# First LayerNorm of a two-layer block: statistics of blocks 2 to 7 moved from VectorE to ScalarE

## The reference, cut to what matters

```python
m = jnp.mean(x, axis=-1, keepdims=True)
v = jnp.var(x, axis=-1, keepdims=True)
xn = (x - m) / jnp.sqrt(v + 1e-5)
x = x + attention(xn) + ffn(xn)
```

## Time and profile before

| | |
|---|---|
| median of 3 runs | 1813.74 us (1809.82 to 1813.79) |
| the profiled execution's own time | 1823.78 us |
| its span on the core | 1821.9 us |
| mean granted TensorE clock | 0.942 of full speed |

### The profile page before, as it was taken

The page is one execution under the profiler, slowest core; times in us unless marked ns, Lnnn a source line. Parts: engine busy times, 40 slices in busy tenths (PEclk is TensorE's granted clock), DMA queues, the critical chain, the costliest instruction groups (busy, mean ns, idle before and its releaser), DMA issues.

```text
span 1821.9 us, 32039 instructions
## 1 busy us (share of the span) xinstructions
PE 1638.2 (90%) x10912; PEld 1214.3 (67%) x10912; DVE 869.7 (48%) x2492; ACT 667.7 (37%) x1617; POOL 738.1 (41%) x845
## 2 busy tenths in 40 slices
PE   3798988988887999999988578999899999999997
PEld 2344534444443799999755345656899999999997
DVE  3866787667650232322165797988322112222221
ACT  1344444445452122222353334432433333333332
POOL 3122223455551055555542237885233333333332
PEclk8789988989897999999999789999999999999999
DMA  7533433252404122222351255435622222222221
GB/s 203 117 90 95 97 84 76 54 106 64 95 5 163 66 72 72 71 73 70 117 162 58 73 174 117 97 70 123 240 36 36 38 36 39 36 36 35 37 40 22
DMA packets 79739, 149.98 MB, mean 82 GB/s; under 512 B 13125, under 2 KB 61377, under 8 KB 73441
## 3 DMA queue, kind: packets, MB, share of 16 engines
q1 hardware_dynamic: 55040, 110.56, 23.2%
q0 software_dynamic: 24544, 37.38, 9.5%
HBM read 103.05 MB, written 44.45 MB: 81 GB/s over the span
## 4 chain that ended last, share of the span: by engine, by line
PE 78%; DVE 12%; issue 4%; ACT 2%; DMA 2%; POOL 1%; SPq 0%; DVEq 0%; ACTq 0%; POOLq 0%
PE PS L1413 21%; PE PS L1431 20%; PE PS L1299 5%; DVE PS L1717 5%; PE PS L1237 3%; PE PS L1526 3%; PE PS L1378 3%; PE PS L1387 2%; PE PS L1263 2%; PE PS L1617 2%; PE PS L1398 2%; PE PS L1284 2%; PE PS L1325 2%; PE PS L1536 1%; PE PS L1606 1%
## 5 line engine op out<-in xcount | busy, mean ns | idle before, releaser
L1413 PEld LDWEIGHTS PS<-arena 128*128 128x128 f32 x3408 | 400.7, 193 | 15.8 <-DVE arena L1940 4.5
L1413 PE MATMUL PS<-arena 128*128 128x128 f32 x3408 | 407.5, 277 | 3.1 <-DVE arena L1940 3.1
L1431 PE MATMUL PS<-arena 128*128 x1704 | 392.4, 379 | 0.0
L1431 PEld LDWEIGHTS PS<-arena 128*128 128x128 f32 x1704 | 311.6, 190 | 40.2 <-issue 0.2
L1940 DVE COPY arena<-PS 128x256 f32<-128x256 f32 x142 | 60.3, 425 | 413.2 <-PE PS L1398 402.9
L1717 DVE CUSTOM_DVE_ANT_0 PS<-PS,arena 128x512 f32<-128x512 f32 (+3 forms) x512 | 234.2, 524 | 36.2 <-PE PS L1263 36.0
L866 POOL DMA_INDIRECT out<-arena x71 | 111.6, 1572 | 313.6 <-ACT arena L1087 292.5
L1077 ACT ACTIVATE arena<-PS,arena 128x128 f32<-128x128 f32 x568 | 162.4, 368 | 138.2 <-PE PS L1413 138.2
L1016 ACT ACTIVATE arena<-PS 128x512 f32<-128x512 f32 (+1 forms) x256 | 166.9, 704 | 89.0 <-PE PS L1284 87.8
L806 POOL TENSOR_SCALAR_AFFINE_SELECT arena<-arena 128x256 f32<-128x256 f32 x256 | 99.0, 411 | 230.8 <-ACT arena L1016 229.4
L852 POOL DMA_INDIRECT arena<-XN,arena x142 | 142.0, 1000 | 122.8 <-PE PS L1398 81.6
(11 more groups left out here) (237 smaller groups left out, 2058.5 us busy)
## 6 DMA issues: line engine op xcount, KB each, us to landing
arena<-FD SPq DMA_DIRECT2D x32, 512.0 KB
arena<-in_w SPq DMA_DIRECT2D x16, 1024.0 KB
SPL<-arena SPq DMA_DIRECT2D x32, 384.0 KB, 2.6
arena<-SPL SPq DMA_DIRECT2D x32, 384.0 KB, 5.3
XN<-arena SPq DMA_DIRECT2D x16, 512.0 KB, 2.9
arena<-SPL SPq DMA_DIRECT2D x32, 256.0 KB, 6.2
arena<-SUM SPq DMA_DIRECT2D x16, 512.0 KB, 5.1
arena<-in_x SPq DMA_DIRECT2D x8, 512.0 KB, 10.1
```

The costliest lines, as they stand in the source:

```text
L1413: ins = pe.matmul(o, m.now[i % 2][:, c * F + 128 * f:c * F + 128 * f + 128], m.xt[i % 2][:, 128 * c:128 * c + 128], start=(c == 0), stop=( ...
L1431: ins = pe.matmul(to, m.hT[i % len(m.hT)][:, 128 * c:128 * c + 128], m.WD[:, bass.ds(e * (nf * 256) + c * 256, 256)], start=(c == 0), stop ...
```

## The change

VectorE keeps the statistics of blocks 0 and 1. Those of blocks 2 to 7 are made by ScalarE at the same places of `plan0`: four `Copy` activations with scale 1/256, whose accumulated sum is the mean, a wait on its own semaphore `mean_made`, and four `Square` activations of `mean - x` (scale -1, the mean as a per-partition bias) whose accumulated sum is 256 times the variance. What the activations write goes to `OTT`, which holds nothing at that time. The last square root takes scale 1/256 to make up for it and waits on `square_made` in place of `stat`. The counts of `stat` fall by 12 in layer 1.

```diff
             def root0(k):
                 lo, hi = ((0, 4), (4, 8), (8, 32))[k]
-                act.wait_ge(stat, (2, 4, 16)[k])
+                if k < 2:
+                    act.wait_ge(stat, 2 * k + 2)
+                else:
+                    act.wait_ge(square_made, NB - 2)
                 act.wait_ge(const_set, 3)
-                act.activation(RS[:, lo:hi], MV[:, lo:hi, 1], ACT.Sqrt, bias=EPS[:, :]).then_inc(root)
+                act.activation(RS[:, lo:hi], MV[:, lo:hi, 1], ACT.Sqrt, bias=EPS[:, :], scale=1.0 if k < 2 else 1.0 / D).then_inc(root)
+
+            def stats0(n):
+
+                left = [OTT[j // 2][:, 256 * (j % 2):256 * (j % 2) + 256] for j in range(4)]
+                act.wait_ge(x_in[n], 16)
+                if n > 2:
+                    act.wait_ge(square_made, n - 2)
+                for j in range(4):
+                    i = 4 * n + j
+                    ins = act.activation(left[j], ACC[:, i, :], ACT.Copy, scale=1.0 / D, accum_out=MV[:, i, 0:1])
+                ins.then_inc(mean_made)
+                act.wait_ge(mean_made, n - 1)
+                for j in range(4):
+                    i = 4 * n + j
+                    ins = act.activation(left[j], ACC[:, i, :], ACT.Square, bias=MV[:, i, 0:1], scale=-1.0, accum_out=MV[:, i, 1:2])
+                ins.then_inc(square_made)
...
             for kind, *a in plan0:
-                if kind == "root":
+                if kind == "stats" and a[0] >= 2:
+                    stats0(*a)
+                elif kind == "root":
...
             for kind, *a in plan0:
-                if kind == "stats":
+                if kind == "stats" and a[0] < 2:
                     stats0(*a)
```

More of the change, by code:

```diff
@@ L500, in build @@
         stat = sem("stat")
+        mean_made, square_made = sem("mean_made"), sem("square_made")
         root = sem("root")
@@ L1113, in scalar @@
                     b = a[0]
-                    act.wait_ge(stat, 16 + 2 * b + 2)
+                    act.wait_ge(stat, 4 + 2 * b + 2)
                     act.activation(RS[:, 4 * b:4 * b + 4], MV[:, 4 * b:4 * b + 4, 1], ACT.Sqrt, bias=EPS[:, :]).then_inc(root)
@@ L1973, in stats1 @@
                 if b:
-                    dve.wait_ge(stat, 16 + 2 * b)
+                    dve.wait_ge(stat, 4 + 2 * b)
                 else:
@@ L1980, in stats1 @@
                 ins.then_inc(stat)
-                dve.wait_ge(stat, 16 + 2 * b + 1)
+                dve.wait_ge(stat, 4 + 2 * b + 1)
                 for j in range(4):
```

## The result

The changed kernel takes 1818.7 us in the median of 22 runs (1811.0 to 1824.5), the kernel before 1811.4 in 22 (1805.5 to 1817.3). The ratio is 1.0038, 95% interval 1.0027 to 1.0049: slower by 6.9 us, 4.9 to 8.9. The forecast was 7.9 us or 0.44%, and a time of 1821.6 us.

A forecast was written before the change was run, and what follows sets the result against it. VectorE bounds the changed stretch before; afterwards ScalarE's chain sets norm(2), 5.8 us later, plus 2.1 us waiting on TensorE's lowered clock: 7.9 us on 1813.7 gives 1821.6 us. Range for 8 in 10: 1815 to 1828.

The forecast's parts named there:

- What bounds the stretch: 60 to 90 us: VectorE bounds it before, 28.07 of 30 us busy; six blocks, 10.3 us, are the most saved.
- VectorE's relief wins: Rival: accumulations overlap so well that a block costs under 2.4 us; faster, at best 10.3 us off, 1803.4; chance 4%.
- Blocks 2 and 3 at no cost: Their 7.7 us fit ScalarE's 15.90 us idle before maxrow(0); block 2 brings the first rounding 1.72 us earlier, to 68.91.
- The price of a block: On ScalarE: four copies, four squares and the rounding of the rows, 3.85 us, against VectorE's 1.72.
- The chain: ScalarE's steps from the first rounding at 68.91, with blocks 4 to 7, put norm(2)'s subtraction at 93.29, +5.8 us.
- extra table load: Rival at blocks 6 and 7: square not in the exponential's table, four switches, 5.2 us more, 1826.8; chance 8%.
- The clock's term: After TensorE's idle stretch, about 73 to 79.6 us, its clock is lower; ScalarE waits 2.1 us for project_v's second copy.
- The sum: At norm(2): 5.8 + 2.1 = 7.9 us late, all of it reaching the end; 1821.6 us, 0.44% slower.
- A sign of being wrong: Behind norm(2): all spans should shift by a constant; a later stage starting less late would make the prediction wrong.
- absorption: Rival, behind norm(2) or by a cheap block: delay partly swallowed, 1815.7 to 1819.5 us; chance 24%.
- The point of no change: Block price on ScalarE at which norm(2) would be neither later nor sooner: 3.85 - 5.83 / 4 = 2.4 us.

The follow-up runs named there:

- two_three: Changed kernel with only blocks 2 and 3 on ScalarE, 4 to 7 back on VectorE: 1810.7 us, ratio 1.0000 to the kernel before.
- warm_longer: Changed kernel with TensorE's two idle stretches filled by 58 and 34 unused matmuls: 1821.8 us, ratio 1.0055 to the kernel before.
- again: The changed kernel unaltered, timed once more with a second trace: 1819.7 us, ratio 1.0050 to the kernel before.
- four_seven: Changed kernel with blocks 2 and 3 back on VectorE, 4 to 7 on ScalarE: 1824.3 us, ratio 1.0053 to the kernel before.
- warm: Changed kernel with TensorE's two idle stretches filled by 40 and 24 unused matmuls: 1820.0 us, ratio 1.0043 to the kernel before.
- squares_only: Changed kernel without the four copies, their wait and the bias, mean taken as 0: 1812.9 us, ratio 0.9998 to the kernel before.
- early4: Changed kernel with blocks 2 to 5 on ScalarE, all at block 2's place, 6 and 7 on VectorE: 1809.7 us, ratio 0.9983 to the kernel before.
- early3: Changed kernel with blocks 2 to 4 on ScalarE, all at block 2's place, 5 to 7 on VectorE: 1808.3 us, ratio 0.9980 to the kernel before.
- early3_again: early3 timed once more for a tighter interval: ratio 0.9991 to the kernel before.

## Why the prediction was right

- **What bounds the stretch.** As predicted, VectorE's relief did not count once ScalarE's chain was the longer one. The 10.3 us taken off VectorE turned into waits: the five between 66 and 96 us add up to 18.0 us (forecast: some 15), 4.46 at the reciprocal among them.
- **A misread chain, without effect on the sum.** The prediction says that the `bn_stats` of all six blocks stand in the chain of the kernel before. Five do. Block 3's, at 66.14, do not: there the chain runs over TensorE and ScalarE, and VectorE waits 1.51 us for the rounding:

```profile
62.05 1.27 DVE arena L1657 x4
...
66.28 0.60 PE PS L1271 x4
66.88 3.72 PE PS L1237 x4
70.63 0.61 ACT arena L993
71.26 0.70 DVE arena L1703
...
72.33 1.41 DVE arena L1657 x4
```

So at most five blocks, 8.6 us, could come off, and not the 10.3 of the rival "VectorE's relief wins". The forecast itself counts only block 2 ahead of the first rounding and adds up ScalarE's steps from there, so it did not need the wrong reading.
- **Blocks 2 and 3 at no cost.** Shown by two_three: -1.5 us at norm(2), forecast -1.7, and block 3 went into a wait. That they cost nothing is clear; how much block 2 gives is within the scatter of the traces ahead of it. That the first rounding stood at 68.91 to the hundredth was luck: maxrow(0) came 1.42 us sooner (65.50), not 1.72, the projection behind it took 3.48 us instead of 3.78, and in the second trace of the same kernel the rounding stood at 69.42.
- **The price of a block.** Forecast 3.85, measured 3.71. The pitch of the copies is 0.40 (0.41 forecast), of the squares 0.49 (0.50). Four blocks make it 0.6 us over. The durations alone have medians of 406 and 492 ns (24 each). The estimates worked out in the prediction from the Trainium skill (ScalarE: Activation LUTs, What ACT_TABLE_LOAD costs) were 399 and 492. The drain of 1.38 us at a switch, which that section also gives, is not in these rows: the load lasted 1.28 us from 92.74, right behind the exponentials, and the root ran at 94.03.
- **The chain.** Forecast 68.91, 73.27, load of the table 77.7, norm(2) 93.29 without the clock; measured 68.91, 73.11, 77.40, and 94.59 - 1.92 = 92.67. No extra table load appeared, so squares run behind an exponential without one; that rival is out. The kernel before spoke against it more than the prediction says: at 974.62 us layer 1's squares follow a Gelu activation (L1058, at 974.12, behind a table load at 972.83) without a load between.
- **The clock's term.** Forecast a wait of 2.1 us, measured 1.92 and, in a second execution, 0.93. warm_longer takes it away and norm(2) follows. So it is a real term of some 1 to 2 us, which depends on the execution; that the first trace met the forecast to 0.2 us is partly luck.
- **The sum.** 7.9 at norm(2), measured 7.1 there (6.7 in the second trace) and 6.9 in the whole (9.1 in the second set). Whether a delay at norm(2) reaches the end, all runs together say, in us against the kernel before:

| kernel | norm(2), one trace | the whole (95% interval) |
|---|---|---|
| changed | +7.1 | +6.9 (4.9 to 8.9) |
| again | +6.7 | +9.1 (6.3 to 11.8) |
| four_seven | +8.4 | +9.6 (6.2 to 13.0) |
| warm | +6.1 | +7.8 (4.9 to 10.7) |
| warm_longer | +5.6 | +10.0 (6.0 to 13.8) |
| squares_only | -0.3 | -0.4 (-4.2 to 3.4) |
| two_three | -1.5 | 0.0 (-3.1 to 3.3) |
| early4 | -2.3 | -3.1 (-6.2 to 0.0) |
| early3 | -4.7 | -3.6 (-6.7 to -0.4) |
| early3_again | -4.9 | -1.6 (-4.5 to 1.1) |

Late kernels are slow and early ones are not, and in eight of ten rows norm(2) lies inside the interval of the whole. So the delay reaches the end in the main, which is shown; to a microsecond or two it is not, and why warm_longer's 2 us did not show stays open.
- **A sign of being wrong that appeared.** The prediction calls itself wrong if a later stage starts less late than norm(2), and expects a constant shift. In the two first traces the last projection was only 5.5 us late and the first routed expert 0.4. I do not count it as absorption, because the medians are 7.3 apart and the second trace of the changed kernel differs from its own first by 5.0 us at that expert. The sign asked of two single traces what they could not tell.
- **What was off.** The profiled execution was to take 1831.7 us and took 1824.35. The reason is the scatter between executions, not the change: the trace of before was one of its slowest executions. A sum put on the median did not suffer from it; one put on the profiled execution did. The forecast of 1821.6 us was 2.9 above the measured 1818.7; 2.3 of that is its base, a median of three runs (1813.7) where 22 gave 1811.4.
- **The point of no change.** Forecast at a block price of 2.4 us. At 1.77 us norm(2) was only 0.3 us sooner, where the same line would give 4 x 0.63 = 2.5. There ScalarE waits for project_v, which the line leaves out. The forecast did not need it, but the price of the rival "VectorE's relief wins" rested on it, and it was too simple.

## What to carry to other kernels

Work moved to an engine that is idle on average has to be priced in the places where it lands: the three blocks that fit a true gap in front of ScalarE's critical steps gave a small gain (3.6 and 1.6 us in two sets, the first clear of zero), the four laid between critical steps cost more at norm(2) than the whole change did. Compare the new price per piece (3.7 us against 1.72) with the slack at each place, in the order in which the engine must execute. And when the expected effect is below a per cent, take the mechanism from an interval inside the trace and the size from many runs; two single spans here showed 0.7 us where the medians showed 7.3.

## What the runs showed of the hardware that was not expected

- An accumulating activation without order to the next has a pitch of 0.40 us for 128x256 (0.49 with a per-partition bias); its 0.19 us accumulator read is followed 0.10 us after its start by the next activation. A block of eight with the semaphore between is 3.71 us, 3.89 when the next block follows at once (51.17 to 55.06), 2.2 times what `bn_stats` and `bn_aggr` need.
- The granted clock fell in the same gap of TensorE in both traces of the changed kernel, but not at the same point: at 74 to 76 us it was 0.81 in the first and 1.00 in the second, at 84 to 86 it was 0.62 and 1.00. ScalarE's wait was 1.92 us in the one and 0.93 in the other. With the gap filled by 58 matmuls the clock was 1.00 from 70 to 96 us, in the one trace taken.
- Two executions of the changed kernel that reached norm(2) within 0.5 us of each other began the first routed expert 5.0 us apart.
